# Moving one quarter's layer-norm statistics from ahead of the transpose loop into it, in an attention and mixture-of-experts kernel

## The chip, the cores and the metric

One Trainium2 chip, all eight cores. Each core runs the same program on its own batch element (2048 tokens of 1024 features) and there is no exchange between cores. The metric is the device time in microseconds of the slowest core.

## The reference

For one core, in short:

```python
xn = layernorm(x)                      # x: 2048 x 1024, no gain, eps 1e-5
qkv = xn @ w_qkv.T                     # w_qkv: 3072 x 1024
attn = causal_softmax(q @ k.T / 8) @ v # 16 heads of 64
logits = xn @ wr + br                  # 4 experts, the best 2 are taken
gates = softmax(top2(logits))
h_e = gelu(xn @ w1[e] + b1[e])         # 1024 -> 4096, all four experts
y_e = h_e @ w2[e] + b2[e]              # 4096 -> 1024
out = x + attn @ w_out.T + sum_k gates_k * (y_sel(k) - c_sel(k) + c_sum)
```

Here c_e is what expert e gives for a zero input. It is a constant row, and its part is small work at the end.

## The kernel before

The program is written out by hand, one instruction stream per engine (SyncE, GpSimd, TensorE, VectorE, ScalarE), with semaphores between the streams. `E` adds an instruction to a stream, `I` adds one that increments a semaphore, `W` adds a wait. So the order in which the Python code emits work is the order of each engine's queue. `P.brk()` closes a block, and all engines meet there.

**Block 0** makes constants, loads small inputs and transposes the biases. It holds one small Ln activation (line 245) that has an activation table loaded early.

**Block 1**, the one that the change touches, does layer norm, transposes and the Q, K and V projections.

- GpSimd's queue issues casting copies of `w_qkv` to a bf16 scratch tensor `wqkv_bf` in HBM, the K part first, then Q, then V, and then of `w_out`. They start when the first two pieces of x are in.
- SyncE's queue loads x into `xA` (two halves for the first quarter, then three quarters), then waits for a part of `wqkv_bf` and issues eight transposing loads of it into `wqkvT` (line 356), 24 in all.
- x is treated in four quarters of 512 tokens (`q_` 0 to 3), each of four tiles of 128 tokens (`ts`). `emit_ln(q_)` emits the statistics: on VectorE a square (line 387), two row sums (390, 393) for each tile and a few small operations; on ScalarE Ln and Exp for the reciprocal root (408, 411); on VectorE the shift `nmr_a` (414).
- The loop over `q_` does for each tile: normalize on ScalarE into `xnf` (433), eight 128x128 transposes on TensorE (442), and their evacuation, even ones on ScalarE (448, 451), odd ones on VectorE (458, 461). Behind the four tiles come the router logits: matmuls (474, 478), an add on VectorE (483), four small transposes (493) and copies into `lgt` on VectorE (497).
- Behind the logits of a quarter the statistics of a later quarter are emitted, and then the K projections that the tokens so far allow (`emit_qk_tt`, matmuls 280 and 285): 4 groups behind quarter 0, 12 behind quarter 1, 8 behind quarter 2 and 8 behind quarter 3. A group is eight 128x512 matmuls into one of four PSUM slots. VectorE evacuates it into `k_fm` (299), and only then the slot can be used again.
- Then all Q groups, evacuated by ScalarE (292), and V.

Before the change the statistics are emitted thus: quarter 0 (in two halves) and quarter 1 ahead of the loop, quarter 2 behind the logits of quarter 0, quarter 3 behind those of quarter 1, none behind those of quarter 2.

**Block 2** is causal attention (matmuls from line 687) with the output projection, **block 3** the experts (line 854 the first matrix, 885 the second), and the **last block** adds x, attention and experts and stores.

Of the kernel before, what the change touches and what calls it, by code (L numbers as in the profile page):

```python
# [9 lines left out]
AF = mybir.ActivationFunctionType  # L10
# [39 lines left out]
def build_nc():  # L50
# [18 lines left out]
    def at(name, shape, dt, off):  # L69
        return nc.alloc_sbuf_tensor_at(name, shape, dt, offset=base + off)  # L70
# [7 lines left out]
    ceps = at("ceps", [128, 1], F32, 1184)  # L78
# [11 lines left out]
    r_a = at("r_a", [128, 16], F32, 2848)  # L90
# [91 lines left out]
    def W(eng, s, v):  # L182
        if v > 0:
            P.emit(eng, lambda e, s=s, v=v: e.wait_ge(sem[s], v))  # L184
# [8 lines left out]
    def I(eng, s, fn, n=1):  # L193
        if n >= 16 and C[s] > 0:
            W(eng, s, C[s])
        C[s] += n
        v = C[s]
        P.emit(eng, lambda e, fn=fn, s=s, n=n: fn(e).then_inc(sem[s], n))
        return v

    def E(eng, fn):
        P.emit(eng, fn)
# [40 lines left out]

    W("scalar", "SG", v_consts)
    E("scalar", lambda s: s.activation(std_a[0:1, 0:1], ceps[0:1, 0:1], AF.Ln))
    W("tensor", "SX", v_small)
    W("tensor", "SG", v_consts)
    v_b1c = [0, 0]
# [127 lines left out]
    def emit_ln(q_, half=None):  # L376
        ks = range(4) if half is None else range(half * 2, half * 2 + 2)
        if q_ != 0:
            W("vector", qsem[q_], v_xq[q_])
        elif half is not None:  # L380
            W("vector", "SXR", v_xh0[half])
        E("vector", lambda v: v.drain())
        for k_ in ks:
            ts = q_ * 4 + k_
            if k_ > ks.start:
                E("vector", lambda v: v.drain())
            E("vector", lambda v, ts=ts: v.tensor_tensor(
                xsq[ts % 4][:], xA[:, ts * 1024:(ts + 1) * 1024],
                xA[:, ts * 1024:(ts + 1) * 1024], ALU.mult))
            E("vector", lambda v, ts=ts: v.tensor_reduce(  # L390
                s1a[:, ts:ts + 1], xA[:, ts * 1024:(ts + 1) * 1024], AX.X, ALU.add))
            E("vector", lambda v: v.drain())
            E("vector", lambda v, ts=ts: v.tensor_reduce(
                s2a[:, ts:ts + 1], xsq[ts % 4][:], AX.X, ALU.add))
        sl = slice(q_ * 4 + ks.start, q_ * 4 + ks.stop)
        E("vector", lambda v: v.drain())
        E("vector", lambda v, sl=sl: v.tensor_scalar_mul(
            m_a[:, sl], s1a[:, sl], 1.0 / 1024.0))
        E("vector", lambda v, sl=sl: v.tensor_scalar_mul(
            E2a[:, sl], s2a[:, sl], 1.0 / 1024.0))  # L400
        E("vector", lambda v: v.drain())
        E("vector", lambda v, sl=sl: v.tensor_tensor(
            mma[:, sl], m_a[:, sl], m_a[:, sl], ALU.mult))
        E("vector", lambda v: v.drain())
        v_var = I("vector", "SV", lambda v, sl=sl: v.tensor_tensor(
            var_a[:, sl], E2a[:, sl], mma[:, sl], ALU.subtract))
        W("scalar", "SV", v_var)
        E("scalar", lambda s, sl=sl: s.activation(
            std_a[:, sl], var_a[:, sl], AF.Ln, bias=ceps[:, 0:1]))
        E("scalar", lambda s: s.drain())  # L410
        v_rstd[q_] = I("scalar", "SS", lambda s, sl=sl: s.activation(
            r_a[:, sl], std_a[:, sl], AF.Exp, scale=cm05[:, 0:1]))
        W("vector", "SS", v_rstd[q_])
        v_nmr = I("vector", "SV", lambda v, sl=sl: v.scalar_tensor_tensor(
            nmr_a[:, sl], m_a[:, sl], -1.0, r_a[:, sl], ALU.mult, ALU.mult))
        v_nmrq[q_] = v_nmr
        v_nmrh[(q_, half)] = v_nmr

    emit_ln(0, half=0)
    emit_ln(0, half=1)  # L420
    emit_ln(1)
    for q_ in range(4):
        for k_ in range(4):
            ts = q_ * 4 + k_
# [62 lines left out]
        for k_ in range(4):  # L487
# [10 lines left out]
                lgt[:, ts * 4:(ts + 1) * 4], trp[0:128, 0:4]))  # L498
            tr_evac[tr_idx] = v_lgt[ts]
            tr_idx += 1  # L500
        if q_ + 2 < 4:
            emit_ln(q_ + 2)
        for fc8 in range(8, 16):
            if tr_evac_chunk[fc8]:
                for tt in range(q_ + 1):
# [32 lines left out]
    for lev in range(2, max(len(tl) for tl in terms.values())):  # L538
        for e_, tl in terms.items():
            if lev < len(tl):  # L540
                q_, k_ = tl[lev]
# [547 lines left out]
```

How the kernel before makes its waits and increments, by code:

```python
    def W(eng, s, v):  # L182
        if v > 0:
            P.emit(eng, lambda e, s=s, v=v: e.wait_ge(sem[s], v))
# [8 lines left out]
    def I(eng, s, fn, n=1):  # L193
        if n >= 16 and C[s] > 0:
            W(eng, s, C[s])
        C[s] += n
        v = C[s]
        P.emit(eng, lambda e, fn=fn, s=s, n=n: fn(e).then_inc(sem[s], n))
        return v
```

## Time and profile before

| what | value |
|---|---|
| median of the timed runs | 3334.38 us (two runs, 3312.66 and 3356.1) |
| time of the profiled execution | 3293.19 us |
| its span, slowest core (core 1) | 3291.7 us |
| spans of the other cores | 3279.8 to 3289.9 us |
| mean granted TensorE clock, all cores | 0.837 to 0.839 |
| TensorE busy | 2824.2 us (86%) |
| VectorE busy | 785.7 us (24%) |
| ScalarE busy | 863.1 us (26%) |

Times in the trace are microseconds from the start of the span. Matmul rows count a run of like instructions as one, with their number behind an x. In square brackets stands how long the engine was idle before the row and what released it. "PE" is TensorE, "PEld" its weight loads, "DVE" VectorE, "ACT" ScalarE, "POOL" GpSimd, "SPq" SyncE's queue of DMA issues.

### The profile page before, as it was taken

The page shows a single profiled execution, that of the slowest core. Times are in us where ns is not written, and L with a number is a line of the kernel's source. Part 1 is how long each engine was busy: PE and PEld are TensorE (multiplying, and loading weights), DVE is VectorE, ACT ScalarE, POOL GpSimd, SP SyncE. Part 2 cuts the span into 40 slices and gives each one's busy share as a digit, 9 for nine tenths or more (in the row PEclk, how much of TensorE's full clock was granted, in tenths as well). Part 3 has the DMA queues.
Part 4 walks back from the last instruction along what each step waited for, and adds up shares of the span by engine and source line. Part 5 has one row for each costly group of instructions (what it writes and reads, how often), then busy time and mean ns, then how long its engine had stood idle before and what let it go on. Part 6 is the DMA issues. An engine that isn't in the chain of part 4 may idle for free. (4 is left out here: it accounts for less than half of the span.)

```text
span 3291.7 us, 30070 instructions; the slowest of 8 cores (3279.8 to 3291.7 us)
## 1 busy us (share of the span) xinstructions
PE 2824.2 (86%) x11124; PEld 1081.2 (33%) x11124; DVE 785.7 (24%) x1057; ACT 863.1 (26%) x1168; POOL 35.7 (1%) x60
## 2 busy tenths in 40 slices
PE   2379867778878885999999999999999999999970
PEld 1134311111111112444444444444444444444420
DVE  5341353322221111111111111111111121111224
ACT  1122154545545552111222111112222111112100
POOL 0000000000000000000000000000000000000000
PEclk9689856565575556999999999999999999999955
DMA  8620000000000105032033123303311330330017
GB/s 148 98 36 1 20 7 26 0 26 0 1 26 1 26 0 102 1 52 45 8 52 52 18 34 52 52 1 52 52 28 25 52 52 2 50 52 1 1 40 266
DMA packets 79693, 127.86 MB, mean 39 GB/s; under 512 B 36158, under 2 KB 36286, under 8 KB 79298
## 3 DMA queue, kind: packets, MB, share of 16 engines
q0 software_dynamic: 33600, 75.50, 15.1%
q1 hardware_dynamic: 45954, 50.44, 5.1%
q8 instruction: 96, 1.57, 0.2%
q14 instruction: 43, 0.35, 0.0%
HBM read 176.26 MB, written 25.17 MB: 61 GB/s over the span
## 5 line engine op out<-in xcount | busy, mean ns | idle before, releaser
L854 PE MATMUL P<-xn_fm,w1g 128*128 128x512 bf16 x4096 | 897.1, 380 | 24.6 <-PEq L43 24.6
L885 PE MATMUL P<-w2g,h_sb 128*128 128x512 bf16 x4096 | 894.3, 379 | 0.0
L862 ACT ACTIVATE h_sb<-P,b_sb 128x512 bf16<-128x512 f32 x512 | 351.8, 687 | 1445.7 <-PE P L854 1445.7
L904 DVE SCALAR_TENSOR_TENSOR accum<-P,agate,accum 128x1024 f32<-128x1024 f32 x240 | 308.2, 1284 | 1379.8 <-PE P L885 1379.8
L854 PEld LDWEIGHTS P<-xn_fm,w1g 128*128 128x128 bf16 x4096 | 400.2, 98 | 513.1 <-issue 35.2
L885 PEld LDWEIGHTS P<-w2g,h_sb 128*128 128x128 bf16 x4096 | 400.7, 98 | 483.4
L701 ACT ACTIVATE p_sb<-P,cneg 128x1024 bf16<-128x1024 f32 x320 | 353.0, 1113 | 402.3 <-PE P L693 401.9
L722 PE MATMUL P<-p_sb,v_ext 128*65 128x512 bf16 x320 | 191.3, 598 | 123.0 <-DVE p_sb L709 65.4
L729 PE MATMUL P<-p_sb,v_ext 128*65 128x512 bf16 x320 | 194.4, 607 | 0.0
L709 DVE TENSOR_TENSOR p_sb<-p_sb,masks 128x1024 bf16<-128x1024 bf16 x128 | 88.0, 690 | 407.2 <-ACT p_sb L701 407.2
L693 PE MATMUL P<-q_fm,k_fm 64*128 64x512 bf16 x320 | 175.7, 608 | 0.0
L687 PE MATMUL P<-q_fm,k_fm 64*128 64x512 bf16 x320 | 168.7, 584 | 7.2 <-DVE proj L769 6.5
L722 PEld LDWEIGHTS P<-p_sb,v_ext 128*65 128x65 bf16 x320 | 41.0, 128 | 378.5 <-issue 377.1
L280 PE MATMUL P<-xn_fm,wqkvT 128*128 128x512 bf16 x448 | 114.0, 397 | 57.5 <-DMA wqkvT<-wqkv_bf 45.8
L687 PEld LDWEIGHTS P<-q_fm,k_fm 64*128 64x128 bf16 x320 | 28.9, 99 | 208.8 <-issue 208.8
L442 PE MATMUL P<-ident,xnf 128*128 128x128 f32 x128 | 32.6, 388 | 68.2 <-ACT xnf L433 65.2
L280 PEld LDWEIGHTS P<-xn_fm,wqkvT 128*128 128x128 bf16 x448 | 44.7, 101 | 115.7 <-issue 68.2
L660 PE MATMUL P<-rbr,ones_bf 1*64 1x512 bf16 x64 | 39.4, 615 | 45.8 <-ACT rbr L654 41.6
L664 DVE COPY rbsb<-P 64x512 f32<-64x512 f32 x64 | 43.7, 683 | 123.9 <-PE P L660 123.7
L756 PE MATMUL P<-w_outT,attn_cat 128*128 128x512 bf16 x240 | 64.9, 431 | 9.6 <-ACT p_sb L701 7.9
L927 PE MATMUL P<-w2g,hfake 128*1 128x512 bf16 x256 | 57.8, 379 | 0.0
L1009 PE MATMUL P<-b2p_sb,aem 4*128 4x512 f32 x64 | 54.9, 1058 | 1.5 <-DVE b2p_sb L998 1.5
(110 smaller groups left out, 940.9 us busy)
## 6 DMA issues: line engine op xcount, KB each, us to landing
w1g<-w POOLq DMA_DIRECT2D x16, 2048.0 KB, 17.7
w2g<-w POOLq DMA_DIRECT2D x16, 2048.0 KB, 28.0
attn_sc<-proj SPq DMA_DIRECT2D x16, 512.0 KB, 2.6
xrg<-x SPq DMA_DIRECT2D x4, 2048.0 KB, 10.0
arg<-attn_sc SPq DMA_DIRECT2D x4, 2048.0 KB, 14.5
y<-outr SPq DMA_DIRECT2D x16, 512.0 KB, 2.9
xA<-x SPq DMA_DIRECT2D x3, 2048.0 KB, 24.8
wqkv_bf<-w_qkv POOLq DMA_DIRECT2D x3, 2048.0 KB, 45.8
```

What stands on the lines that cost most here:

```text
L280: t.matmul(pt[:, off:off + 512], wqkvT[:, dc * 3072 + fc8 * 128:dc * 3072 + (fc8 + 1) * 128], xn_fm[:, dc * 2048 + tt * 512:dc * 2048 + (t ...
L687: E("tensor", lambda t, kb0=kb0, pb=pb, hr=hr, pair=pair, qt=qt: t.matmul(pb[:, 0:512], k_fm[hr:hr + 64, pair * 2048 + kb0 * 128:pair * 20 ...
L693: t.matmul(pb[:, 512:1024], k_fm[hr:hr + 64, pair * 2048 + (kb0 + 1) * 128:pair * 2048 + (kb0 + 2) * 128], q_fm[hr:hr + 64, pair * 2048 + ...
L701: ve = I("scalar", "SS", lambda s, pb=pb, psb=psb: s.activation(psb[:], pb[:, 0:1024], AF.Exp, bias=cneg8[:, 0:1]))
L709: vm = I("vector", "SV", lambda v, psb=psb, j=j: v.tensor_tensor(psb[:], psb[:], masks[:, j * 1024:(j + 1) * 1024], ALU.mult))
L722: E("tensor", lambda t, p=p, head=head, psb=psb, sl=sl: t.matmul(sl[0:65, :], bass.AP(v_ext, 2 * p * VW + head * 65, [[NTS * VW, 128], [1, ...
L729: psb=psb, sl=sl, av_stop=av_stop: t.matmul(sl[0:65, :], bass.AP(v_ext, (2 * p + 1) * VW + head * 65, [[NTS * VW, 128], [1, 65]]), psb[:, ...
L756: t.matmul(pb[:, half * 512:(half + 1) * 512], ac[:, ec * 512 + ts4 * 128:ec * 512 + (ts4 + 1) * 128], w_outT[:, ec * 1024 + half * 512:ec ...
L854: t.matmul(PH67[par][:, 0:512], w1g[buf][:, dc * 1024 + hc * 128:dc * 1024 + (hc + 1) * 128], xn_fm[:, dc * 2048 + tt * 512:dc * 2048 + (t ...
L862: s.activation(h_sb[tt % 2][:, hc * 512:(hc + 1) * 512], PH67[par][:, 0:512], AF.Gelu, bias=b1_sb[:, e_ * 32 + g_ * 8 + hc:e_ * 32 + g_ * ...
L885: pt=pt, st=st, sp=sp: t.matmul(pt[:, half * 512:(half + 1) * 512], h_sb[tt % 2][:, hc * 512 + ts4 * 128:hc * 512 + (ts4 + 1) * 128], w2g[ ...
L904: v.scalar_tensor_tensor(accum[:, tsg * 1024:(tsg + 1) * 1024], pt[:, 0:1024], agate[:, tsg * 4 + e_:tsg * 4 + e_ + 1], accum[:, tsg * 102 ...
```

## The change

The statistics of quarter 1 are no longer emitted ahead of the loop. Behind the logits of quarter `q_` the loop emits the statistics of quarter `q_ + 1` in place of `q_ + 2`. So quarter 1 stands behind the logits of quarter 0, quarter 2 behind those of quarter 1, quarter 3 behind those of quarter 2. In block 0 a second small activation, an Exp, follows the Ln. No instruction but that one is added, and none is removed.

```diff
@@ -243,6 +243,7 @@
     W("scalar", "SG", v_consts)
     E("scalar", lambda s: s.activation(std_a[0:1, 0:1], ceps[0:1, 0:1], AF.Ln))
+    E("scalar", lambda s: s.activation(r_a[0:1, 0:1], ceps[0:1, 0:1], AF.Exp))
     W("tensor", "SX", v_small)
@@ -418,7 +419,6 @@
     emit_ln(0, half=0)
     emit_ln(0, half=1)
-    emit_ln(1)
     for q_ in range(4):
@@ -498,8 +498,8 @@
             tr_idx += 1
-        if q_ + 2 < 4:
-            emit_ln(q_ + 2)
+        if q_ + 1 < 4:
+            emit_ln(q_ + 1)
         for fc8 in range(8, 16):
```

## Rows read from the trace of the kernel before

**Rows 1.** The page: span, and busy time of each engine.

```profile
span 3291.7 us, 30070 instructions; the slowest of 8 cores (3279.8 to 3291.7 us)
...
PE 2824.2 (86%) x11124; PEld 1081.2 (33%) x11124; DVE 785.7 (24%) x1057; ACT 863.1 (26%) x1168; POOL 35.7 (1%) x60
```

**Rows 2.** Waits of TensorE to 285 us: total, times, longest (us).

```profile
PE P L280 <- DMA wqkvT<-wqkv_bf: 45.8, 3, 41.8
PE P L280 <- DVE k_fm L299: 10.2, 1, 10.2
```

**Rows 3.** Busy time by stretch; the last three: granted clock, DMA share, GB/s.

```profile
40.00:60.00 20.00, 3.52 (x13) 2.32 (x13) 14.55 (x26) 5.40 (x16) 0.00 (x0) 1.00 1.01 121
60.00:80.00 20.00, 14.33 (x38) 5.09 (x38) 5.89 (x24) 6.74 (x23) 0.00 (x0) 1.00 1.00 122
80.00:100.00 20.00, 0.38 (x2) 0.24 (x2) 15.52 (x21) 1.72 (x3) 0.00 (x0) 0.57 1.00 121
```

**Rows 4.** Timeline: end of quarter 0's statistics, first normalize of quarter 0.

```profile
36.38 0.16 DVE L414 SCALAR_TENSOR_TENSOR nmr_a<-m_a,r_a 128x2 f32<-128x2 f32 x1 [0.87 <-ACT r_a L411]
...
53.32 1.22 ACT L433 ACTIVATE xnf<-xA,nmr_a,r_a 128x1024 f32<-128x1024 f32 x1
```

**Rows 5.** Timeline: last work of quarter 0 on VectorE, then the first K groups.

```profile
79.84 0.86 DVE L497 COPY lgt<-P 128x4 f32<-128x4 f32 x4 [0.58 <-PE P L493]
...
122.23 3.14 PE L280 MATMUL P<-xn_fm,wqkvT 128*128 128x512 bf16 x7 [41.80 <-DMA wqkvT<-wqkv_bf]
```

**Rows 6.** VectorE behind quarter 1: first and last operation of the statistics.

```profile
162.55 1.22 DVE L387 TENSOR_TENSOR xsq<-xA 128x1024 f32<-128x1024 f32 x1
...
179.01 0.16 DVE L414 SCALAR_TENSOR_TENSOR nmr_a<-m_a,r_a 128x4 f32<-128x4 f32 x1 [0.86 <-ACT r_a L411]
```

**Rows 7.** TensorE behind quarter 1: groups 1, 4 (its last matmul), 5 and 9.

```profile
162.65 1.67 PE L280 MATMUL P<-xn_fm,wqkvT 128*128 128x512 bf16 x7 [0.46 <-DVE lgt L497]
...
169.33 0.38 PE L285 MATMUL P<-xn_fm,wqkvT 128*128 128x512 bf16 x1
...
179.95 3.15 PE L280 MATMUL P<-xn_fm,wqkvT 128*128 128x512 bf16 x7 [10.24 <-DVE k_fm L299]
...
189.51 1.67 PE L280 MATMUL P<-xn_fm,wqkvT 128*128 128x512 bf16 x7
```

**Rows 8.** Timeline behind quarter 2: logits, groups 1 and 2, quarter 3's first transposes.

```profile
222.13 0.86 DVE L497 COPY lgt<-P 128x4 f32<-128x4 f32 x4 [0.59 <-PE P L493]
223.21 3.14 PE L280 MATMUL P<-xn_fm,wqkvT 128*128 128x512 bf16 x7 [0.49 <-DVE lgt L497]
...
226.45 1.68 PE L280 MATMUL P<-xn_fm,wqkvT 128*128 128x512 bf16 x7
...
238.54 0.60 PE L442 MATMUL P<-ident,xnf 128*128 128x128 f32 x4
```

**Rows 9.** Timeline of ScalarE and VectorE: table loads and end of block 0.

```profile
6.79 1.28 ACT L245 ACT_TABLE_LOAD   x1 [6.79 <-POOL masks L236]
8.08 0.20 ACT L245 ACTIVATE std_a<-ceps 1x1 f32<-1x1 f32 x1
...
10.08 0.32 DVE L255 COPY b_sb<-P 128x32 f32<-128x32 f32 x2 [0.43 <-PE P L252]
...
25.04 1.28 ACT L408 ACT_TABLE_LOAD   x1 [16.75 <-DVE var_a L405]
```

**Rows 10.** Core 4, lines 280, 687, 854: duration min/median/max, first and last start.

```profile
L280 PE MATMUL P<-xn_fm,wqkvT x448: 376/379/635, 117.8 to 328.3; 128*128 128x512 bf16 x150
L687 PE MATMUL P<-q_fm,k_fm x320: 372/603/607, 397.9 to 1232.9; 64*128 64x512 bf16 x160
L854 PE MATMUL P<-xn_fm,w1g x4096: 378/379/632, 1285.7 to 3082.7; 128*128 128x512 bf16 x196
```

**Rows 11.** Core 1, lines 687 and 854: as in rows 10.

```profile
L687 PE MATMUL P<-q_fm,k_fm x320: 372/603/607, 402.9 to 1238.0; 64*128 64x512 bf16 x160
L854 PE MATMUL P<-xn_fm,w1g x4096: 379/379/631, 1292.7 to 3090.4; 128*128 128x512 bf16 x196
```

**Rows 12.** Busy time by stretch, as in rows 3: behind quarter 3, and the experts.

```profile
266.00:400.00 134.00, 125.03 (x579) 56.30 (x577) 37.45 (x146) 26.38 (x49) 0.00 (x0) 0.98 0.03 7
...
1400.00:3150.00 1750.00, 1742.38 (x7992) 778.60 (x7991) 325.71 (x258) 327.06 (x476) 24.52 (x28) 0.99 0.21 34
```

## The prediction
> **What bounds the kernel now.** I first read the page. TensorE is busy for 2824.2 of 3291.7 us, no other engine for a third of that [rows 1]. The change touches only the first 400 us, so the mean says little. I next read TensorE's waits in the part up to 285 us, since the work that the change moves lies there. Two of them matter [rows 2]. The K groups wait 45.8 us in all for the transposing loads of the weights, 41.8 us of it in one piece, and they wait 10.2 us once for VectorE to evacuate `k_fm`. The reader is to see that the first is a wait for data that no layer norm takes part in, and that the second is a wait for an engine.
>
> The stretches between 40 and 100 us then show why the first wait is there: the 16 DMA engines are fully busy (share 1.00 to 1.01) in all three [rows 3], whether VectorE has 14.55, 5.89 or 15.52 us of work in the stretch. That is the casting of the weights, and behind it their transposing loads. Nothing in that chain waits for the statistics: the casts wait for the first pieces of x, the transposing loads for the casts.
>
> Last I read the timeline around each place where the statistics stand or will stand. From 266 us on TensorE is busy 125.03 of 134 us, and in the experts 1742.38 of 1750 us [rows 12]. What comes late at the end of quarter 3 is therefore late at the end.
>
> **The change, part by part.**
>
> *Ahead of quarter 0.* Quarter 0's statistics are done at 36.38 + 0.16 = 36.54 us, but the first normalize of quarter 0 starts at 53.32 us [rows 4]. In between lie quarter 1's statistics, on VectorE's queue ahead of quarter 0's evacuations and on ScalarE's queue (Ln and Exp, which wait for VectorE) ahead of quarter 0's normalize. Taking them out starts quarter 0 at about 36.6 us, 53.32 - 36.6 = 16.7 us earlier, and its logits end at about 80.70 - 16.7 = 64.0 us in place of 79.84 + 0.86 = 80.70 [rows 5].
>
> What is next after that is the first K group, and it starts at 122.23 us, released by the weights' DMA [rows 5]. It will start there again. The earlier quarter 0 only lengthens the wait of 41.8 us to about 58.5 us. I take the gain on the path as 0. Bounds: 0 if the DMA keeps its time, 16.7 us if the landing came earlier by all of that.
>
> *Behind quarter 0.* Quarter 2's statistics go out of this place and quarter 1's come in, the same 12 large operations. They take 179.17 - 162.55 = 16.6 us by their like [rows 6], thus run from 64 to 80.7 us, in VectorE's idle time before the first K group is to be evacuated at about 126 us. Cost 0. The cover is the DMA wait, about 41 us of it is left. Were it gone, the four K groups would just fit the four slots and quarter 1's evacuations would come up to 16.6 us late.
>
> *Behind quarter 1.* Quarter 3's statistics go out and quarter 2's come in. The shape, the place and the work behind it are the same. The wait of 10.24 us [rows 7] stays. Cost 0.
>
> *Behind quarter 2.* Here nothing stood, and now quarter 3's statistics stand on VectorE's queue ahead of the eight K evacuations. This is the cost, and it has its like one quarter earlier. There the statistics start at 162.55 [rows 6], TensorE fills its four slots from 162.65 to 169.33 + 0.38 = 169.71, stands, and goes on at 179.95 [rows 7]. So TensorE resumes 179.95 - 162.55 = 17.4 us after the statistics begin. And groups 5 to 8 then take 189.51 - 179.95 = 9.56 us, though a group in steady flow takes (238.54 - 226.45) / 7 = 1.73 us, four of them 6.9 us [rows 8]. The 2.65 us more are two groups at the lower clock after the pause: seven matmuls of group 5 take 3.15 us, those of group 9 1.67 us [rows 7], nearly the two levels, 1.2 and 2.4 GHz.
>
> Laid on quarter 2: logits done at 222.13 + 0.86 = 222.99 [rows 8], statistics start at 222.99 + 0.09 = 223.08 (the gap is 162.55 - 162.46 one quarter before). TensorE resumes at 223.08 + 17.4 = 240.48, four groups take 9.56, and quarter 3's transposes begin at 250.04 in place of 238.54 [rows 8]. That is **11.5 us** later. Check by parts: groups 1 to 4 take 3.24 + 3 x 1.73 = 8.43 us and end at 231.64, so the wait is 8.84 us, and 8.84 + 2.65 = 11.5.
>
> What else is queued behind the statistics? On VectorE only the `k_fm` copies. On ScalarE, Ln and Exp and then the normalizes of quarter 3, ready at about 241 us, before TensorE needs them at 250. SyncE and GpSimd have no work there, and no DMA issue is moved.
>
> Bounds of this term: group 1 behind quarter 2 ran at the lower clock (3.24 us [rows 8], 1.73 in flow). On a core where it runs at the higher one the kernel before is 1.5 us shorter there, while VectorE sets the same resumption after, which makes the loss 13.0 us. If the two slow groups after the pause don't come, it is 8.8 us.
>
> *The added Exp.* ScalarE loads a table at 6.79 us, runs Ln to 8.28, and loads again at line 408, 1.28 us, though that too is Ln [rows 9]. The added Exp costs 0.2 to 1.28 + 0.2 = 1.48 us in block 0, thus to 9.76 us at most, under the end of the last bias copy at 10.40 [rows 9], which covers it. Without that cover x and the casts would start up to 1.5 us later, and so would everything that the DMA sets. If the load at line 408 goes, quarter 0 starts 1.28 us earlier still, ahead of the same DMA wait. I take 0; bounds 0 to +1.5.
>
> *Behind quarter 3.* The shift runs into Q, V, attention and the experts. Their work isn't changed, and the loads of expert weights are released by TensorE's progress, so they shift too. How strictly does a shift pass? Core 4 starts its K groups at 117.8 and attention at 397.9, 4.4 and 5.0 us before core 1, and takes 1285.7 - 397.9 = 887.8 us up to the experts [rows 10] where core 1 takes 889.8 [rows 5, 11]. So it passes within about 2 us.
>
> **Sum.** 0 + 0 + 0 + 11.5 + 0 = +11.5 us on the profiled execution's own 3293.19 us, so 3304.7 us. That is +0.35%. The timed runs lie higher, 3312.66 and 3356.1, their median 41.2 us above the profiled execution. A shift of 11.5 us on that median gives **3345.9 us**.
>
> **The rivals.**
>
> *Faster, since the weights land earlier.* The place is the wait at 122.23 us. If its release moved with quarter 0, the gain there would be 16.7 us, and the sum 11.5 - 16.7 = -5.2 us, 3288.0 on the profiled time and 3329.2 on the median. It decides once the landing comes more than 11.5 us earlier. For it: less VectorE work lies between 80 and 122 us. Against it: the DMA share stays at 1.00 to 1.01 and the throughput at 121 or 122 GB/s with VectorE at 5.89 us of 20 or at 15.52 [rows 3].
>
> *The weights land later.* Quarter 0's copies move from 55 to 70 us down to 38 to 53 us, onto the casts. Those are 16 times two of about 0.28 us on VectorE, some 9 us. Had the DMAs to stand for them, 9 us would come on top: 3313.7, on the median 3354.9. The stretch 40 to 60 holds the first of them and shows no loss of DMA share [rows 3]. The Trainium skill, page SBUF — State Buffer, in the part on DVE blocking DMA, has a rule of this kind: copies on VectorE in its two-port mode keep GpSimd from writing the descriptors of DMAs that it issues, and such are the casts. By that rule alone a loss could appear here; by the rows the queue is full rather than starved.
>
> *No change.* The statistics behind quarter 2 cost nothing if the K groups didn't need VectorE. Time 3293.2, median 3334.4. Against it: the same work stalls TensorE for 10.24 us one quarter before [rows 7].
>
> *Slower by over 2%.* That needs 67 us. No place in the first block is that long; only the experts are, by a lower granted clock: 1742.38 us busy at 0.99 [rows 12] would have to run at 0.99 x 1742 / 1809 = 0.953. Time 3360, median 3401. For it speaks nothing but that the stage is long. Against it: cores 4 and 1 reach it 7.0 us apart and take 3082.7 - 1285.7 = 1797.0 and 1797.7 us from their first to their last group [rows 10, 11].
>
> **How the numbers follow.** The forecast has 0.86, faster by an earlier landing 0.03, a later landing 0.04, no change 0.05, slower by the clock 0.02. About 2% is what a measurement of this kernel tells from no change. The first four lie within it. The two runs of the kernel before lie 1.3% apart, so I leave 0.01 on either side for scatter: faster 0.01, same 0.96, slower 0.03. The mechanism's own range is +8 to +15 us (8.8 to 13.0, and 2 us for the passage). The range of the time has to hold the executions' scatter, which is larger: low is the profiled execution plus 8, 3301 us, high the slower timed run plus 13, 3369 us. The other cases within 2% lie inside it or a few us off it.
>
> **What would show each step.** Right: the first K group still at about 122 us after a wait of some 58 us; quarter 0's first normalize at 35 to 37 us; two waits of TensorE for `k_fm`, of about 10 and 9 us, in place of one; quarter 3's first transposes near 250 us; attention's start some 11.5 us later on each core against the first K group. Wrong: a first K group off 122 us by more than the 4.4 us that cores differ by; no second wait; or a difference that arises behind 400 us.

## The result, and the profile after

The changed kernel takes 3310.32 us (median of 37 runs) against 3296.67 us of the kernel before (36 runs). The ratio is **1.0039, 95% interval 1.0032 to 1.0045**: 0.39% slower, by 3296.67 x 0.0039 = 12.9 us (10.5 to 14.8). That is far under 2%, yet with so many runs the loss is clear of noise. The medians are over all executions; the ratios, here and below, leave out those in which the cores of a die ran at a lower clock, six of each kernel above 3600 us among them.

The page of the changed kernel shows a longer span with the same work, as before to be read against [rows 1]; its slowest core is core 4.

```profile
span 3308.7 us, 30071 instructions; the slowest of 8 cores (3285.3 to 3308.7 us)
...
PE 2826.1 (85%) x11124; PEld 1081.6 (33%) x11124; DVE 785.2 (24%) x1057; ACT 863.5 (26%) x1169; POOL 35.6 (1%) x60
```

Busy times moved by 2 us at most, TensorE's by 1.9. So most of the loss is idle time. The waits of TensorE in the first 296 us of the changed kernel (total, times, longest, as in [rows 2]):

```profile
PE P L281 <- DMA wqkvT<-wqkv_bf: 62.5, 4, 57.6
PE P L442 <- ACT xnf L433: 47.9, 13, 27.3
PE P L281 <- DVE k_fm L300: 18.8, 2, 10.2
```

Two things are to be seen. The wait for the weights has grown from 41.8 to 57.6 us in its longest piece. And there are two waits for `k_fm`, of 8.6 and 10.2 us, where there was one. The line numbers of the K matmuls and copies are one higher than before (281, 286, 300).

The timeline of TensorE in the changed kernel, from the end of quarter 0's logits to the first K group, then groups 1 to 8 behind quarter 2 and the first transposes of quarter 3, answers to [rows 5, 8]:

```profile
63.18 0.89 PE L493 MATMUL P<-ident,lgt_em 4*128 4x4 f32 x4 [1.14 <-DVE lgt_em L483]
121.69 3.15 PE L281 MATMUL P<-xn_fm,wqkvT 128*128 128x512 bf16 x7 [57.63 <-DMA wqkvT<-wqkv_bf]
...
221.19 1.67 PE L281 MATMUL P<-xn_fm,wqkvT 128*128 128x512 bf16 x7 [0.50 <-DVE lgt L497]
...
227.88 0.38 PE L286 MATMUL P<-xn_fm,wqkvT 128*128 128x512 bf16 x1
238.46 3.15 PE L281 MATMUL P<-xn_fm,wqkvT 128*128 128x512 bf16 x7 [10.20 <-DVE k_fm L300]
241.40 0.63 PE L286 MATMUL P<-xn_fm,wqkvT 128*128 128x512 bf16 x1
241.82 2.87 PE L281 MATMUL P<-xn_fm,wqkvT 128*128 128x512 bf16 x7
...
248.20 0.60 PE L442 MATMUL P<-ident,xnf 128*128 128x128 f32 x4
```

Quarter 0 ends 16 us sooner and nothing comes of it: the first K group stands at 121.69. Behind quarter 2 four groups fill the slots, TensorE stands for 10.20 us, and two slow groups follow. VectorE shows what it waits for: the first and last operation of quarter 3's statistics, then the four copies that had been held up.

```profile
221.05 1.23 DVE L388 TENSOR_TENSOR xsq<-xA 128x1024 f32<-128x1024 f32 x1
...
237.52 0.17 DVE L415 SCALAR_TENSOR_TENSOR nmr_a<-m_a,r_a 128x4 f32<-128x4 f32 x1 [0.86 <-ACT r_a L412]
237.62 2.48 DVE L300 CAST k_fm<-P 128x512 bf16<-128x512 f32 x4
```

To compare kernels I cut TensorE's timeline of every core into phases, each from its first row to the first row of the next, and take the median of the eight cores. The K phases of quarters 0, 1 and 2 (us), which hold the waits, with the start of the first K group (range over the cores) ahead of them:

| kernel | first K group | K behind q0 | K behind q1 | K behind q2 |
|---|---|---|---|---|
| before | 117.8 to 122.2 | 13.6 | 32.8 | 13.8 |
| changed | 117.1 to 121.7 | 13.7 | 32.7 | 26.9 |
| e3_all_behind_q0 | 116.3 to 119.7 | 16.7 | 21.5 | 14.3 |
| e4_twice_q3 | 115.6 to 119.9 | 13.2 | 32.7 | 42.4 |
| e5_twice_q1_ahead | 116.5 to 121.0 | 13.2 | 32.7 | 13.8 |
| e6_gate_before | 79.5 to 82.5 | 17.7 | 33.9 | 15.2 |
| e7_gate_after | 62.4 to 65.2 | 18.3 | 33.8 | 25.7 |
| e8_halves | 115.2 to 119.3 | 13.3 | 22.0 | 13.8 |
| e9_gate_halves | 62.3 to 65.4 | 10.8 | 25.0 | 18.0 |
| e10_gate_tiles | 62.4 to 65.7 | 10.8 | 22.5 | 15.0 |

One of these phases differs between the kernel before and the changed one: 26.9 - 13.8 = 13.1 us behind quarter 2. Within the interval of 10.5 to 14.8 us that accounts for the loss. Attention starts 280.2 us behind the first K group in the kernel before and 292.4 us behind it in the changed one (medians of the cores), a shift of 12.2 us.

### The profile page after: what moved, and what is told of

The parts are those of the page before. It is cut to its first block and busy times, and to the rows that moved or that the text cites. A ratio compares the mean times of both kernels' runs of the same rounds, so it can differ in the third digit from the quotient of the medians.

```text
span 3308.7 us, 30071 instructions; the slowest of 8 cores (3285.3 to 3308.7 us)
## 1 busy us (share of the span) xinstructions
PE 2826.1 (85%) x11124; PEld 1081.6 (33%) x11124; DVE 785.2 (24%) x1057; ACT 863.5 (26%) x1169; POOL 35.6 (1%) x60
## 3 DMA queue, kind: packets, MB, share of 16 engines
q0 software_dynamic: 33600, 75.50, 15.3%
## 5 line engine op out<-in xcount | busy, mean ns | idle before, releaser
L722 PE MATMUL P<-p_sb,v_ext 128*65 128x512 bf16 x320 | 191.1, 597 | 123.2 <-DVE p_sb L709 65.7
L756 PE MATMUL P<-w_outT,attn_cat 128*128 128x512 bf16 x240 | 65.7, 435 | 9.6 <-ACT p_sb L701 7.9
## 6 DMA issues: line engine op xcount, KB each, us to landing
xrg<-x SPq DMA_DIRECT2D x4, 2048.0 KB, 10.5
```

The costliest lines, as they stand in the source:

```text
L722: E("tensor", lambda t, p=p, head=head, psb=psb, sl=sl: t.matmul(sl[0:65, :], bass.AP(v_ext, 2 * p * VW + head * 65, [[NTS * VW, 128], [1, ...
L756: t.matmul(pb[:, half * 512:(half + 1) * 512], ac[:, ec * 512 + ts4 * 128:ec * 512 + (ts4 + 1) * 128], w_outT[:, ec * 1024 + half * 512:ec ...
```

## The experiments

**The added Exp alone, and the changed kernel without it.**

```diff
--- before
+++ e1_exp_only
     E("scalar", lambda s: s.activation(std_a[0:1, 0:1], ceps[0:1, 0:1], AF.Ln))
+    E("scalar", lambda s: s.activation(r_a[0:1, 0:1], ceps[0:1, 0:1], AF.Exp))
--- after
+++ e2_no_exp
     E("scalar", lambda s: s.activation(std_a[0:1, 0:1], ceps[0:1, 0:1], AF.Ln))
-    E("scalar", lambda s: s.activation(r_a[0:1, 0:1], ceps[0:1, 0:1], AF.Exp))
```

> The kernel before with only the added Exp activation. Theory (the cost lies in the statistics behind quarter 2): ratio 1.000, no table load more or less, first K group unchanged. Rival (the added activation costs, through a later start of block 1 or another table load): up to 1.5 us in the span, ratio up to 1.0005, and a load of 1.28 us that comes or goes on ScalarE.

> The changed kernel without the Exp activation. Theory: ratio to the kernel before as with it, 1.0039 (+12.9 us). Rival (Exp carries part of the cost): below 1.0034.

Measured: 1.0001 (0.9991 to 1.0011) with Exp alone, 1.0037 (1.0024 to 1.005) for the changed kernel without it. ScalarE's timeline in e1_exp_only, from its start to the first use of the statistics:

```profile
6.79 1.28 ACT L245 ACT_TABLE_LOAD   x1 [6.79 <-POOL masks L236]
8.09 0.20 ACT L245 ACTIVATE std_a<-ceps 1x1 f32<-1x1 f32 x1
8.20 0.18 ACT L246 ACTIVATE r_a<-ceps 1x1 f32<-1x1 f32 x1
24.75 1.28 ACT L409 ACT_TABLE_LOAD   x1 [16.36 <-DVE var_a L406]
```

Ln and Exp run on one load, and the load ahead of line 409 stays. The added activation costs its 0.18 us in cover and spares nothing. The interval of e2 leaves a part of up to 5 us open by time alone; the phases settle it, since the K phase behind quarter 2 is 26.3 us without the Exp and stays at 13.8 us with the Exp alone.

**Is it the place behind quarter 2?** All statistics go under the wait for the weights, and, the other way round, quarter 3's are emitted twice at their new place.

```diff
--- after
+++ e3_all_behind_q0
-        if q_ + 1 < 4:
-            emit_ln(q_ + 1)
+        if q_ == 0:
+            emit_ln(1)
+            emit_ln(2)
+            emit_ln(3)
--- after
+++ e4_twice_q3
         if q_ + 1 < 4:
             emit_ln(q_ + 1)
+        if q_ == 2:
+            emit_ln(3)
```

> The changed kernel with the statistics of quarters 1, 2 and 3 all behind the logits of quarter 0, from 64 to about 114 us, none behind quarters 1 and 2. Theory (each set behind quarter 1 or 2 stalls TensorE and brings slow groups behind it; under the DMA wait a set is free): no wait of TensorE for k_fm above 2 us, 11 to 13 us faster than the kernel before, ratio 0.9962 (0.9955 to 0.9970), and 24 to 26 us faster than the changed one. Rival (the loss comes from the later start of later stages, another clock phase or DMA timing): ratio within 0.002 of 1.

> The changed kernel with the statistics of quarter 3 emitted twice behind quarter 2. Theory: TensorE's wait there grows by one set, 16.6 us, from about 9 to about 26 us, the slow groups behind it stay two; +29 us to the kernel before, ratio 1.0089 (1.0080 to 1.0098). Rival (the loss is not proportional to VectorE's time there): the addition is below 8 us, ratio below 1.0065.

e4_twice_q3 came out at 1.0093 (1.007 to 1.0115), against 1.0089 expected. Its one wait behind quarter 2 is 26.9 us, one set of 16.7 us more than 10.2:

```profile
PE P L281 <- DVE k_fm L300: 36.7, 3, 26.9
```

The phase grew from 26.9 to 42.4 us. A second set of 16.6 us thus costs 15.5 us. It is less than the wait grew by because on six of the eight cores one slow group follows this wait, where two followed on five of eight in the changed kernel. So the loss grows with VectorE's time at that place, nearly one for one once the four slots are full.

e3_all_behind_q0 came out at 0.9974 (0.9963 to 0.9985): faster than both, but 8.6 us faster than the kernel before, not the 12.5 that I expected, and outside the range I gave. Both waits for `k_fm` did go, and the K phase behind quarter 1 fell by 11.3 us. But the one behind quarter 0 grew by 3.1 us. The timelines of core 1 show why: VectorE with the first operation of quarter 3's set and the copies behind it, then ScalarE and TensorE:

```profile
114.81 1.22 DVE L388 TENSOR_TENSOR xsq<-xA 128x1024 f32<-128x1024 f32 x1 [18.82 <-DMA xA<-x]
...
131.76 2.48 DVE L300 CAST k_fm<-P 128x512 bf16<-128x512 f32 x4
```

```profile
130.89 0.30 ACT L409 ACTIVATE std_a<-var_a,ceps 128x4 f32<-128x4 f32 x1 [35.16 <-DVE var_a L406]
...
131.46 1.23 ACT L433 ACTIVATE xnf<-xA,nmr_a,r_a 128x1024 f32<-128x1024 f32 x1
```

```profile
129.28 0.38 PE L286 MATMUL P<-xn_fm,wqkvT 128*128 128x512 bf16 x1
132.93 0.68 PE L442 MATMUL P<-ident,xnf 128*128 128x128 f32 x4 [3.27 <-ACT xnf L433]
```

The fourth quarter of x lands only at 114.8 us, behind the last cast, which lands at some 111 us (28.99 + 81.9). VectorE stood 18.8 us for it and came to the copies at 131.76 us, when the four K groups were already done. The four slots took all of quarter 0's groups, so TensorE didn't wait for the copies. What held up quarter 1 is ScalarE's queue. Quarter 3's Ln and Exp stand on it ahead of quarter 1's first normalize, and they waited for VectorE. On all eight cores TensorE's wait ahead of quarter 1's first transposes is one for `xnf`, of 2.6 to 3.5 us; in the changed kernel there is none. "Idle under the DMA wait" was true of the engine and not of the data. I had looked neither at when each load of x lands nor at what stands behind the statistics on ScalarE.

**Is an earlier start of quarter 0 worth anything?** Here it is made 16.6 us later.

```diff
--- before
+++ e5_twice_q1_ahead
     emit_ln(0, half=1)
     emit_ln(1)
+    emit_ln(1)
```

> The kernel before with the statistics of quarter 1 emitted twice ahead of the loop, so that quarter 0 starts 16.6 us later (near 70 us) instead of 16.7 us earlier. Theory (the DMA wait covers it): TensorE's wait for the weights falls from about 41 to about 24 us, the first K group stays at 116 to 122 us, ratio 1.000 (0.999 to 1.001). Rival (an earlier start of quarter 0 is worth something): +16 us or a part of it, ratio up to 1.005.

Measured 1.0006 (0.9996 to 1.0017): no loss that can be told from none. The two waits of the slowest core:

```profile
PE P L280 <- DMA wqkvT<-wqkv_bf: 24.9, 2, 23.3
PE P L280 <- DVE k_fm L299: 11.5, 2, 10.2
```

The longest wait for the weights is 57.6 us in the changed kernel, 41.8 before, 23.3 here, and the first K group stays within 115 to 122 us in all of them. Over 33 us, the start of quarter 0 doesn't move the first K group.

**What sets the DMA wait, and what does the new order do without it?** The Q, V and `w_out` casts are held back behind the K loads, in the kernel before and in the changed one.

```diff
--- before, after
+++ e6_gate_before, e7_gate_after
     for g_ in (1, 0, 2):
+        if g_ == 0:
+            W("gpsimd", "SQT", 16 * 8)
         I("gpsimd", "SCB%d" % g_, lambda g, g_=g_: g.dma_start(
```

> The kernel before, with the casting copies of the Q and V weights and of w_out held back on GpSimd's queue until the eight transposing loads of the K weights have landed. Theory (the K loads are late because they share full DMA queues with those casts): first K group at 81 to 84 us, right behind quarter 0's logits, quarter 1's transposes near 100 us; 30 to 38 us faster, ratio 0.989 (0.988 to 0.991). Rival (the transposing loads are slow by themselves): first K group above 110 us, ratio above 0.997.

> The changed kernel with the same holding back of casts. Theory: with the DMA wait gone the earlier quarter 0 is worth about its 16.7 us and the wait behind quarter 2 still costs about 13, so it is 2 to 6 us faster than the kernel before with the same casts, ratio to the kernel before 0.988. Rival (the order of the statistics is a loss whatever bounds the start): 10 us or more slower than the kernel before with the same casts, ratio above 0.992.

Measured: e6_gate_before 0.9905 (0.9891 to 0.9919), e7_gate_after 0.99 (0.9871 to 0.9929). The busy shares of e6_gate_before between 60 and 80 us, with clock, DMA share and GB/s at the end, against [rows 3]:

```profile
60.00:80.00 20.00, 14.40 (x37) 4.76 (x36) 5.53 (x22) 6.65 (x22) 0.00 (x0) 1.00 0.40 88
```

The DMA engines are busy for 0.40 instead of 1.00 there, and the first K group starts right behind the logits, at 79.5 to 82.5 us. On the slowest core:

```profile
79.95 0.89 PE L495 MATMUL P<-ident,lgt_em 4*128 4x4 f32 x4 [1.14 <-DVE lgt_em L485]
81.19 1.67 PE L282 MATMUL P<-xn_fm,wqkvT 128*128 128x512 bf16 x7 [0.36 <-DVE lgt L499]
```

So the K loads were late since they shared full DMA engines with casts that nobody needed yet. The same held for x: the slowest of its five loads landed 102.4 us after its issue on the slowest core of the kernel before, and lands after 43.2 us here. The K groups start some 38 us earlier, of which 31 us arrive at the end; the three K phases in the table take 6.6 us more together. In e7_gate_after the first K group starts at 62.4 to 65.2, some 17 us earlier still:

```profile
64.21 1.46 PE L283 MATMUL P<-xn_fm,wqkvT 128*128 128x512 bf16 x6 [0.57 <-DVE lgt L499]
...
68.91 2.50 PE L283 MATMUL P<-xn_fm,wqkvT 128*128 128x512 bf16 x7 [3.03 <-DMA wqkvT<-wqkv_bf]
```

Here the earlier start is kept and the wait behind quarter 2 gives some of it back (25.7 against 15.2 us). The times of the two can't be told apart by their intervals, so the gain of 2 to 6 us that I expected isn't shown by time. In the profiled executions the new order is no longer a loss: 17 gained, 10.5 given back, and the last Q group at 288 to 293 us against 294 to 298.

**Where can the statistics stand at no cost?** First without the change to the casts, then with it.

```diff
--- after
+++ e8_halves
+        if q_ in (1, 2):
+            emit_ln(3, half=q_ - 1)
         W("vector", "ST", v_rt)
...
-        if q_ + 1 < 4:
-            emit_ln(q_ + 1)
+        if q_ == 0:
+            emit_ln(1)
+            emit_ln(2)
```

> The changed kernel with the statistics of quarters 1 and 2 behind quarter 0's logits and those of quarter 3 in two halves, each under the router matmuls of quarter 1 and of quarter 2, where VectorE waits 9 us for TensorE. Theory: no wait of TensorE for k_fm over 2 us and no wait behind the fourth K group of quarter 0 either; K groups of quarter 1 in 21 us rather than 33; 11 us faster than the kernel before, ratio 0.9966 (0.9958 to 0.9974). Rival (work on VectorE anywhere in the loop costs its time): a router phase longer by 8 us in both quarters, ratio above 0.999.

Measured 0.9965 (0.9952 to 0.9978), as expected, with no wait for `k_fm` among the waits of its slowest core. VectorE's timeline there shows the half fitting under the router matmuls but for some 0.4 us (the last of them ends at 155.67 us):

```profile
146.91 1.23 DVE L388 TENSOR_TENSOR xsq<-xA 128x1024 f32<-128x1024 f32 x1
...
155.93 0.16 DVE L415 SCALAR_TENSOR_TENSOR nmr_a<-m_a,r_a 128x2 f32<-128x2 f32 x1 [0.86 <-ACT r_a L412]
156.03 0.74 DVE L485 TENSOR_SCALAR lgt_em<-P,br_em 4x512 f32<-4x512 f32 x1
```

```diff
--- e7_gate_after
+++ e9_gate_halves
+        if q_ < 3:
+            emit_ln(q_ + 1, half=0)
         W("vector", "ST", v_rt)
...
-        if q_ + 1 < 4:
-            emit_ln(q_ + 1)
+        if q_ < 3:
+            emit_ln(q_ + 1, half=1)
--- e9_gate_halves
+++ e10_gate_tiles   (emit_ln also takes a range of tiles)
-        if q_ < 3:
-            emit_ln(q_ + 1, half=1)
+        if q_ == 0:
+            emit_ln(1, half=1)
+        elif q_ < 3:
+            emit_ln(q_ + 1, tiles=range(2, 3))
+        n_k = 0
...
+                        n_k += 1
+                        if n_k == 4 and q_ in (1, 2):
+                            emit_ln(q_ + 1, tiles=range(3, 4))
```

> The changed kernel with the casts held back, and the statistics of quarter q+1 in two halves: the first under the router matmuls of quarter q, the second behind its logits. Theory: a half is 9.2 us, four slots last 6.9 us, so the wait of TensorE for k_fm shrinks from 9 to 10 us to about 3 us each; K groups of quarters 0, 1, 2 in about 12, 25 and 18 us (18, 34 and 26 without the halves); ratio 0.983 (0.981 to 0.985). Rival (a wait of any length costs the slow groups in full, and the first half lengthens the router phase): ratio above 0.987.

> As e9_gate_halves, but in quarters 1 and 2 the second half goes tile by tile, one tile (about 5 us) behind the logits, one behind the fourth K group. Theory: each piece is shorter than the 6.9 us that four slots last, so no wait of TensorE for k_fm over 2 us is left; K groups of quarters 1 and 2 in 21 and 14 us; another 6 to 8 us, ratio 0.981 (0.979 to 0.983). Rival (the pieces still stall since the evacuations catch up too slowly): same as e9_gate_halves within 2 us.

Measured: 0.9828 (0.9811 to 0.9845) and 0.9805 (0.979 to 0.9821), both as expected. The waits for `k_fm` of the slowest core, first of e9_gate_halves:

```profile
PE P L283 <- DVE k_fm L302: 5.5, 2, 2.8
```

and of e10_gate_tiles:

```profile
PE P L283 <- DVE k_fm L302: 0.2, 1, 0.2
```

A piece of 9.2 us against four slots of 6.9 us leaves 2.8 us, where the plain difference is 2.3; the pieces under 6.9 us leave 0.2 us. That is not yet everything: behind quarter 2 the phase of e10_gate_tiles is 15.0 us against 13.8, and on its slowest core TensorE waits 1.05 us there for quarter 3's first normalize, which stands behind the last piece of the statistics. It takes 3226.95 us, 2% less than the kernel before, with the same matrix work in it.

## Why the prediction was right or wrong

**The mechanism was right.** *Ahead of quarter 0:* worth 0, as forecast. The first normalize came at 36.66 us on the slowest core, the first K group at 121.69 us after a wait of 57.6 us (forecast: 36.6, 122, 58.5). *Behind quarters 0 and 1:* nothing changed, phases of 13.7 and 32.7 us against 13.6 and 32.8. *Behind quarter 2:* a second wait and slow groups behind it; quarter 3's transposes begin at 248.20 us (forecast: 250). Attention starts 12.2 us later against the first K group (forecast: 11.5).

**The term of the sum was a little small.** I forecast 11.5 us, the phase grew by 13.1. The step behind it is the one that took the slowest core as the model. On that core group 1 behind quarter 2 ran at the lower clock [rows 8], which hides 1.5 us of the loss. Three of the eight cores were like that before (phases of 15.3 to 15.4 us), the other five had 13.6 to 13.8. The bound that I worked out for these, 13.0 us, was the better value. The sum also joined what doesn't occur together: the short wait of a core whose group 1 is slow (8.84 us) and the two slow groups of a core whose group 1 is at full clock (2.65 us, from [rows 7]). In the profiled executions of both kernels each of the 13 waits with a slow group 1 ahead of it lasts 8.6 to 8.8 us and has one slow group behind it, and each of the 11 with a group 1 at full clock lasts 10.2 us and has two. So a core like the model loses 25.7 - 15.3 = 10.4 us, the others 27.0 - 13.8 = 13.2. Why one or two follow is open.

**The passage to the end** is looser than the 2 us that two cores suggested. From the first attention matmul to the experts the kernel before takes 887.8 to 891.2 us, the changed one 885.7 to 894.1. The medians, 890.6 and 891.8, differ by 1.2 us.

**The steps that failed are the last two.** First, the statement "same". I took 2% as what can be told from no change and so gave 0.96 to "same", for a shift that I had put at +0.35% from a row that shows it. With 37 and 36 runs the interval is 0.06% wide to either side. The measured 0.39% lies inside that forecast of the shift and clear of noise: the statement should have been "slower, by 0.2 to 0.5%". Second, the level. I added the shift to the median of two timed runs, 3334.38, of which one was at 3356.1. The 36 runs put that median at 3296.67. The profiled execution, 3293.19, was the better base: 3304.7 us by my own sum, 5.6 us from the measured median, where 3345.9 is 35.6 us off. Of the 5.6 us, 3.5 are the base (3296.67 against 3293.19) and 1.6 the term behind quarter 2. That the time lay inside the range says little, since the two timed runs had made the range 68 us wide.

**The rivals.** *Weights land earlier:* no; the first K groups start within 117.1 to 121.7 against 117.8 to 122.2. *Weights land later by VectorE's copies:* no. The stretch from 40 to 60 us of the changed kernel now holds quarter 0's copies,

```profile
40.00:60.00 20.00, 13.64 (x39) 5.64 (x38) 6.41 (x28) 9.15 (x30) 0.00 (x0) 1.00 0.98 119
```

and its DMA share and throughput are 0.98 and 119 GB/s against 1.01 and 121 [rows 3], with the first K group no later. The Trainium skill's rule on VectorE blocking DMA (SBUF — State Buffer, the part on DVE blocking DMA) is about VectorE's two-port mode and gives fp32 copies from SBUF to SBUF as its case. Quarter 0's copies come out of PSUM, so I had stretched the rule; this trace shows no loss for them. *No change:* refuted by the interval. *Slower by the clock:* no, the experts run as before, 1743.82 us busy at a granted 1.00 between 1400 and 3150 us (1742.38 at 0.99 before).

**The Exp** shows no cost and no gain, as taken.

## What to carry to other kernels

Moving work earlier pays only if the next thing that is waited for gets earlier too: read what releases the first row behind the gap. Work may stand on a busy queue as long as each piece is shorter than the buffers between the engines last (here four PSUM slots, 6.9 us); cut it so before moving it whole. A hole in an engine's time is usable only from when its input has landed, and what waits for that work on another engine's queue waits with it. A DMA wait ahead of a stage can be made by other transfers that could go later, as it was here.

## What the runs showed of the hardware

- How many groups are slow behind a wait differs. In one execution (core 4 of the changed kernel) the wait of 8.56 us behind quarter 1 brought one slow group (3.31 us), the wait of 10.20 us behind quarter 2 two (3.36 and 2.93), against 1.73 us in steady flow. The cores fall into two patterns, 25.3 to 25.7 and 26.8 to 27.0 us for the same phase: the former with a slow first group, the latter without. With the casts held back (e6 and e7, behind quarter 1) three waits of 10.2 us had one slow group behind them, so the pairing isn't strict.
- Three casting copies of `w_qkv` and one of `w_out`, issued by 34 us, go with full DMA engines from 40 to 100 us (share 1.00 to 1.01 before). A load of x that was issued ahead of them, by 17.2 us, lands at 114.8 us (e3_all_behind_q0, core 1). With three of the four held back, the slowest load of x lands 41.3 to 43.4 us after its issue (e6_gate_before, all cores), against 99.5 to 102.4 us in the kernel before.
- ScalarE loads a table (1.28 us at 24.75 us in e1_exp_only) ahead of the first Ln of block 1, though block 0 ended with Ln and Exp on one load.
